# Feed-forward norm of an attention stack: token rows by two turnings instead of mean products, with the later steps moved back

## The chip, the cores and the metric

The kernel runs on one core of a Trainium2 chip. The metric is the device time of one execution in microseconds (us): 4307.7 us as the median of three runs (4302.38 to 4309.49).

## The reference

Eight modules work in turn on a residual x of 8 sequences of 256 tokens with 128 channels. Two of the eight are a stack of six layers, and nearly all of the time goes there. A layer of the stack is a local attention (16 heads of 64, windows of 32 keys) and a feed-forward block:

```
def shift_tokens(t):          # the upper 64 channels come from the token before
    a, s = jnp.split(t, 2, -1)
    s = jnp.pad(s, ((0, 0), (1, 0), (0, 0)))[:, :-1]
    return jnp.concatenate([a, s], -1)

def ffn_layer(x, g, bln, W1, b1, W2, b2):
    mu = x.mean(-1, keepdims=True)
    var = ((x - mu) ** 2).mean(-1, keepdims=True)
    xn = (x - mu) / jnp.sqrt(var + 1e-05) * g + bln
    hg = xn @ W1 + b1
    a, gate = jnp.split(hg, 2, -1)
    return a * jax.nn.gelu(gate, approximate=False) @ W2 + b2

for i in range(DEPTH):        # 6
    x = attn_layer(shift_tokens(x), Wqkv[i], q_scale[i], k_scale[i], Wo[i]) + x
    x = ffn_layer(shift_tokens(x), ln_g[i], ln_b[i], W1[i], b1[i], W2[i], b2[i]) + x
```

The change is in the first three lines of `ffn_layer`.

## The kernel before

Activations lie with the 128 channels on the partitions and the tokens along the row, in float32. The stack works on pairs of sequences, 512 tokens at a time: 4 pairs a layer, 6 layers, 2 calls, so 48 pairs. A pair takes eight steps, s = 0 to 7, and one step starts one unit, which is one sequence with one group of four heads. Every engine runs its own list of instructions, written out by hand in the `*_stack_step` functions, and engines wait for each other through the counters in `S`. Within a step the units are staggered: the step that starts unit s also carries unit s-2 (its rotated heads are turned), s-3 (scores and softmax) and s-4 (outputs).

TensorE (PE) does in a step, in this order: scores of s-3 (L291, L300), outputs of s-4 (L317), the turning of the heads of s-2 (L421, eight transposes, which wait for GpSimd's `rotated`), query and key products of s (L333, which wait for `scaled` of s-1), value products (L374), the turning of the probabilities (L406) and of the outputs (L391). In steps 3 and 7 the output projection (L361) follows.

What unit s needs before its heads can be turned two steps later runs through four engines: ScalarE (ACT) squares the products (L488), VectorE (DVE) sums them (L614), ACT makes the inverse length (L501, L504), DVE multiplies (L621, `scaled`), and GpSimd (POOL) rotates (L692, L694, L697, `rotated`).

The feed-forward block of a pair is fitted into the steps of the next one. A step has three places for it (`pe_stack_hidden`, `act_stack_hidden`, `dve_stack_hidden`, called with place 0, 1, 2), and `st.ffn(s)` says which step it is. On PE place 0 is before L333, place 1 after L374 and place 2 at the end of the step. On ACT place 0 is before L488, place 1 after the value copy L518 and place 2 at the end. On DVE place 1 is before L614 and place 2 at the end. Before the change:

- step 4: ACT copies the shifted tokens to `h.xc`; PE place 1 multiplies by `mean_w` (L433); DVE place 2 subtracts (L644); ACT place 2 squares (L551)
- step 5: PE place 0 takes the mean of the squares (L437); ACT place 0 makes the factor by Ln and Exp over 512 columns (L554, L556); DVE place 1 multiplies (L647); ACT place 2 applies gain and bias (L560)
- step 6: PE places 0, 1, 2 form the three gate products (L462), and ACT places 0, 1, 2 take them out (L565)
- step 7 and steps 0 to 2 of the next pair: gelu (L569, L571), value products, second product (L456), residual

All products of the block share PSUM bank 7. After the last pair of each call the block runs once more with nothing beside it (`*_stack_drain`).

Of the kernel before, what the change touches and what calls it, by code (L numbers as in the profile page):

```python
# [8 lines left out]
ALU = mybir.AluOpType  # L9
# [242 lines left out]
def stack_buffers(M):  # L252
# [4 lines left out]
                         total=(8,), inv=(8,), o=(8, DH), rs=(NB,)))  # L257


def stack_hidden(M):  # L260

    f = Parts()
    f.xc, f.gate = M.xc[:, 0:NB], M.xc[:, NB:4 * NB].rearrange("p (c t) -> p c t", c=3)
    f.sq, f.hid = M.ln_sq[:, 0, :], M.ln_sq[:, 1:4, :]
    f.rs = stack_buffers(M).rs
    f.ot = M.ln_rs[:].rearrange("p a t -> p (a t)").rearrange("p (g h t) -> p g h t", g=G, h=2)
    return f
# [158 lines left out]
def pe_stack_hidden(M, st, place):  # L426

    pe, S, w, h, s = st.eng, M.st, M.w, stack_hidden(M), st.s
    if st.ffn(4) and place == 1:
# [3 lines left out]
        pe.matmul(bank(M, 7), M.mean_w[:], h.xc, start=True, stop=True).then_inc(S.ffn_moment, 1)  # L433
    if st.ffn(5) and place == 0:
        done = st.ffn_done()
        pe.wait_ge(S.ffn_squared, done + 1)
        pe.matmul(bank(M, 7), M.mean_w[:], h.sq, start=True, stop=True).then_inc(S.ffn_moment, 1)  # L437
    if st.ffn(6):
        c = place
# [13 lines left out]
    if st.ffn(2) and place == 1:  # L453
# [3 lines left out]
        last.then_inc(S.ffn_out, 1)  # L457

# [80 lines left out]
def act_stack_hidden(M, st, place):  # L539
# [9 lines left out]
    if st.ffn(4) and place == 2:  # L549
        act.wait_ge(S.ffn_centred, st.ffn_done() + 1)  # L550
        nc.scalar.activation(h.sq, h.xc, ACT.Square).then_inc(S.ffn_squared, 1)  # L551
    if st.ffn(5) and place == 0:
        act.wait_ge(S.ffn_moment, st.ffn_done() * 2 + 2)
        nc.scalar.activation(h.rs, bank(M, 7), ACT.Ln, bias=M.eps[:, 0:1]).then_inc(S.ffn_scale, 1)  # L554
        act.wait_ge(S.ffn_scale, st.ffn_done() * 2 + 1)
        nc.scalar.activation(bank(M, 7), h.rs, ACT.Exp, scale=-0.5).then_inc(S.ffn_scale, 1)  # L556
    if st.ffn(5) and place == 2:
        act.wait_ge(S.w_ffn, 16 * 4 * (st.ffn_layer() + 1))
        act.wait_ge(S.ffn_normed, st.ffn_done() + 1)
        nc.scalar.activation(h.xc, h.xc, ACT.Identity, bias=w.vecs[:, 1:2], scale=w.vecs[:, 0:1]).then_inc(S.ffn_ready, 1)  # L560
    if st.ffn(6):
        c = place
# [4 lines left out]
    if st.ffn(7) and place == 1:  # L567
# [4 lines left out]
        nc.scalar.preload_act_table_set(NAT)  # L572

# [62 lines left out]
def dve_stack_hidden(M, st, place):  # L636
# [5 lines left out]
    if st.ffn(4) and place == 2:  # L642
        dve.wait_ge(S.ffn_moment, done * 2 + 1)
        nc.vector.tensor_tensor(h.xc, h.xc, bank(M, 7), ALU.subtract).then_inc(S.ffn_centred, 1)  # L644
    if st.ffn(5) and place == 1:
        dve.wait_ge(S.ffn_scale, done * 2 + 2)
        nc.vector.tensor_tensor(h.xc, h.xc, bank(M, 7), ALU.mult).then_inc(S.ffn_normed, 1)  # L647
# [59 lines left out]
def pe_stack_drain(M, pe, t):  # L707
# [3 lines left out]
    pe.matmul(bank(M, 7), M.mean_w[:], h.xc, start=True, stop=True).then_inc(S.ffn_moment, 1)  # L711
    pe.wait_ge(S.ffn_squared, t.done + 1)
    pe.matmul(bank(M, 7), M.mean_w[:], h.sq, start=True, stop=True).then_inc(S.ffn_moment, 1)
# [20 lines left out]
def act_stack_drain(M, act, t):  # L734
# [7 lines left out]
    act.wait_ge(S.ffn_centred, t.done + 1)  # L742
    nc.scalar.activation(h.sq, h.xc, ACT.Square).then_inc(S.ffn_squared, 1)
    act.wait_ge(S.ffn_moment, t.done * 2 + 2)
    nc.scalar.activation(h.rs, bank(M, 7), ACT.Ln, bias=M.eps[:, 0:1]).then_inc(S.ffn_scale, 1)
    act.wait_ge(S.ffn_scale, t.done * 2 + 1)
    nc.scalar.activation(bank(M, 7), h.rs, ACT.Exp, scale=-0.5).then_inc(S.ffn_scale, 1)
# [1150 lines left out]
```

## Time and profile before

| what | value |
|---|---|
| median of three runs | 4307.7 us |
| the profiled execution | 4315.31 us, span 4313.5 us |
| PE matmul busy | 3889.5 us (90%) |
| DVE busy | 2743.1 us (64%) |
| ACT busy | 2678.2 us (62%) |
| POOL busy | 3002.4 us (70%) |
| TensorE clock granted, 700 to 1800 us | 1.00 |

Busy times are shares of the whole span. Matmuls are pipelined, so a busy PE still has to be read from the starts of its instructions. In the timelines one row is a run of instructions of one line, with its start, its length from the first start to the last end, and in brackets how long the engine was idle before it and what ended that.

### The profile page before, as it was taken

To read this page: it belongs to the slowest core of one execution; us is meant where nothing else is said; L and a number is where in the kernel's file an instruction comes from. 1 tells how busy PE (TensorE), PEld (TensorE's weight loads), DVE (VectorE), ACT (ScalarE), POOL (GpSimd) and SP (SyncE) were. 2 spreads that over 40 slices of the span, in tenths; PEclk is the share of its full clock that TensorE was granted. 3 is DMA by queue.
4 is the path that set the end of the run, shared out by engine and by line. 5 is a ranking of instruction groups with operands and counts; after the bars stand their busy time and mean duration, and the time that the engine had idled before them with its cause. 6 is when DMAs were issued, how large, how long until landed. Compare 5 with 4: busy or idle time off the path is not lost.

```text
span 4313.5 us, 165583 instructions
## 1 busy us (share of the span) xinstructions
PE 3889.5 (90%) x69444; PEld 2741.9 (64%) x69444; DVE 2743.1 (64%) x4939; ACT 2678.2 (62%) x5554; POOL 3002.4 (70%) x1858
## 2 busy tenths in 40 slices
PE   7989999999999999977999999999999998375976
PEld 4556666766666767645666676767676765153645
DVE  5666766667676767645766666767676765624741
ACT  5657666676766767644666676767666675133752
POOL 0088888888888888825888888888888885611011
PEclk9999999999999999989999999999999999677987
DMA  2033433433334334312334343333433432040004
GB/s 69 2 83 92 110 97 96 111 93 104 104 93 108 99 102 105 91 54 53 95 101 105 89 112 95 102 106 94 109 99 95 111 93 57 0 114 19 2 13 128
DMA packets 349777, 367.29 MB, mean 85 GB/s; under 512 B 58737, under 2 KB 285298, under 8 KB 348786
## 3 DMA queue, kind: packets, MB, share of 16 engines
q1 hardware_dynamic: 338834, 348.59, 30.9%
q8 instruction: 555, 9.09, 0.9%
q0 software_dynamic: 2048, 4.20, 0.3%
q10 hardware_dynamic: 8160, 3.93, 0.3%
q14 instruction: 180, 1.47, 0.1%
HBM read 246.79 MB, written 109.71 MB: 83 GB/s over the span
## 4 chain that ended last, share of the span: by engine, by line
PE 39%; DVE 4%; ACT 3%; issue 3%; POOL 2%; DMA 1%; POOLq 0%; DVEq 0%; ACTq 0%
PE banks L333 6%; PE banks L361 4%; PE banks L374 4%; PE banks L421 3%; PE banks L462 3%; PE banks L317 3%; PE banks L300 2%; PE banks L406 2%; PE banks L391 2%; PE banks L456 1%; PE banks L1457 1%; ACT arena L1071 1%; PE banks L1477 1%; DVE arena L621 1%; PE banks L998 1%
## 5 line engine op out<-in xcount | busy, mean ns | idle before, releaser
L692 POOL TENSOR_TENSOR arena<-arena 128x512 f32<-128x512 f32 x768 | 959.5, 1270 | 394.0 <-DVE arena L621 253.6
L697 POOL TENSOR_TENSOR arena<-arena 128x1024 f32<-128x1024 f32 x384 | 905.9, 2359 | 30.1
L694 POOL TENSOR_TENSOR arena<-arena 128x1024 f32<-128x1024 f32 x384 | 908.1, 2365 | 0.0
L621 DVE SCALAR_TENSOR_TENSOR arena<-arena,banks 128x512 f32<-128x512 f32 x768 | 493.7, 684 | 508.7 <-ACT arena L504 502.1
L333 PE MATMUL banks<-w_qk,arena 128*128 128x512 f32 x1536 | 736.0, 602 | 16.4 <-DVE arena L797 10.6
L472 ACT COPY arena<-banks 128x512 f32<-128x512 f32 x384 | 224.5, 585 | 645.4 <-PE banks L421 645.2
L614 DVE TENSOR_REDUCE arena<-arena 128x8 f32<-128x512 f32 x768 | 487.6, 671 | 83.6 <-ACT arena L488 83.5
L488 ACT ACTIVATE arena<-banks 128x512 f32<-128x512 f32 x768 | 441.4, 593 | 66.3 <-PE banks L333 52.6
L333 PEld LDWEIGHTS banks<-w_qk,arena 128*128 128x128 f32 x1536 | 276.9, 193 | 272.5 <-issue 272.5
L421 PE MATMUL banks<-ident,arena 128*128 128x128 f32 x3072 | 423.1, 281 | 19.4 <-POOL arena L697 19.3
L588 DVE TENSOR_REDUCE arena<-banks 128x8 f32<-128x512 f32 x384 | 264.2, 688 | 212.6 <-PE banks L317 211.6
L374 PE MATMUL banks<-w_v,arena 128*128 128x256 f32 x1536 | 395.0, 380 | 0.0
L317 PE MATMUL banks<-arena 64*32 64x64 f32 x24576 | 341.8, 224 | 56.5 <-issue 55.4
L374 PEld LDWEIGHTS banks<-w_v,arena 128*128 128x128 f32 x1536 | 285.7, 191 | 160.8 <-issue 140.8
L421 PEld LDWEIGHTS banks<-ident,arena 128*128 128x128 f32 x3072 | 332.1, 142 | 56.0 <-POOL arena L697 21.9
L361 PE MATMUL banks<-ln_rs,w_o 128*128 128x256 f32 x1536 | 349.1, 380 | 1.4 <-ACT ln_rs L536 1.4
L317 PEld LDWEIGHTS banks<-arena 64*32 64x32 f32 x24576 | 280.0, 105 | 86.4 <-issue 67.3
L300 PE MATMUL banks<-arena 64*32 64x64 f32 x24576 | 325.3, 222 | 0.0
L526 ACT COPY arena<-banks 128x512 f32<-128x512 f32 x384 | 227.1, 591 | 148.9 <-PE banks L406 143.2
L361 PEld LDWEIGHTS banks<-ln_rs,w_o 128*128 128x128 f32 x1536 | 292.8, 191 | 42.0 <-ACT ln_rs L536 1.8
L604 DVE TENSOR_REDUCE arena<-arena 128x8 f32<-128x512 f32 x384 | 263.5, 686 | 64.5 <-ACT arena L481 24.5
L300 PEld LDWEIGHTS banks<-arena 64*32 64x32 f32 x24576 | 298.8, 105 | 0.2
(240 smaller groups left out, 6511.2 us busy)
## 6 DMA issues: line engine op xcount, KB each, us to landing
v_rows<-arena SPq DMA_DIRECT2D x1536, 64.0 KB
arena<-v_rows SPq DMA_DIRECT2D x768, 128.0 KB, 2.6
arena<-v_rows SPq DMA_DIRECT2D x768, 112.0 KB, 2.4
arena<-in_moe_w SPq DMA_DIRECT2D x30, 515.5 KB, 3.8
w_qk<-in_stack_qk SPq DMA_DIRECT2D x48, 256.0 KB, 3.0
w_v<-in_stack_v SPq DMA_DIRECT2D x48, 128.0 KB, 3.4
w_o<-in_stack_o SPq DMA_DIRECT2D x12, 512.0 KB
w_w<-in_stack_w SPq DMA_DIRECT2D x12, 341.0 KB, 3.1
```

The costliest lines, as they stand in the source:

```text
L300: last = pe.matmul(bank(M, 4 + par)[c:c + 32, o:o + KW], f.q[r, u % 2, hp, 32 * win:32 * win + 32], f.k[r, u % 2, hp, 32 * win:32 * win + ...
L317: last = pe.matmul(bank(M, 4 + par)[c:c + 32, o:o + DH], f.pt[r, win // 4, hp, c:c + 32], f.vb[r, u % 2, win, hp, :], start=True, stop=True)
L333: pe.matmul(bank(M, tile), f.sh[:, (s // G) % 2, o:o + 128], w.qk[:, g], start=True, stop=True).then_inc(S.qk, 1)
L361: last = pe.matmul(y, w.o[:, 2 * g + hp, :], stack_hidden(M).ot[:, g, hp, :], start=(g == 0 and hp == 0), stop=(g == G - 1 and hp == 1))
L374: last = pe.matmul(bank(M, 2)[:, 2 * D * tile:2 * D * tile + 2 * D], f.sh[:, (s // G) % 2, o:o + 128], w.v[:, g].rearrange("p a c -> p (a ...
L421: last = pe.transpose(bank(M, 2 if qk else 3)[:, o:o + 128], f.rot[:, u % 2, 2 * tile + qk, 2 * hp:2 * hp + 2, :], M.ident[:])
L488: nc.scalar.activation(f.sq[:, tile].rearrange("p h q d -> p (h q d)"), bank(M, tile), ACT.Square).then_inc(S.squared, 1)
L614: last = nc.vector.tensor_reduce(f.length[:, tile], f.sq[:, tile], AX.X, ALU.add)
L621: last = nc.vector.scalar_tensor_tensor(qn[:, :, tile], rn, 1e12, bank(M, tile).rearrange("p (h q d) -> p h q d", h=GH, q=2), ALU.min, ALU ...
L692: nc.gpsimd.tensor_tensor(f.sined[:, :, :, half, :], x[:, :, :, 1 - half, :], sines[:, :, mine].unsqueeze(1).to_broadcast([D, GH, 4, DH // ...
L694: nc.gpsimd.tensor_tensor(rot, x.rearrange("p h t a d -> p h t (a d)"), cosines.unsqueeze(1).to_broadcast([D, GH, 4, DH]), ALU.mult).then_ ...
L697: nc.gpsimd.tensor_tensor(rot, rot, f.sined.rearrange("p h t a d -> p h t (a d)"), ALU.add).then_inc(S.rotated, 1)
```

## The change

The norm is computed in token rows. PE turns the four blocks of 128 tokens of `h.xc` into rows (four transposes at the place of the first mean product). DVE reads them from bank 7 with four `bn_stats` and four `bn_aggr`, which give mean and variance of each token in a column. ACT makes the factor from 4 columns instead of 512. DVE writes the four normed blocks with one `tensor_scalar` each. PE turns them back at place 0 of step 6, and ACT applies gain and bias while it takes them out of bank 7. The gate products each move one place later: to places 1 and 2 of step 6 and place 0 of step 7. The square, the subtraction and both mean products go. The drains get the same operations in the same order.

```diff
@@ pe_stack_hidden
-        pe.matmul(bank(M, 7), M.mean_w[:], h.xc, start=True, stop=True).then_inc(S.ffn_moment, 1)
-    if st.ffn(5) and place == 0:
-        done = st.ffn_done()
-        pe.wait_ge(S.ffn_squared, done + 1)
-        pe.matmul(bank(M, 7), M.mean_w[:], h.sq, start=True, stop=True).then_inc(S.ffn_moment, 1)
-    if st.ffn(6):
-        c = place
+        pe_hidden_rows(M, pe)
+    if st.ffn(6) and place == 0:
+        pe.wait_ge(S.ffn_normed, st.ffn_done() + 1)
+        pe_hidden_turned(M, pe)
+    if st.ffn(6) and place > 0 or st.ffn(7) and place == 0:
+        c = (place + 2) % 3
...
+def pe_hidden_rows(M, pe):
+    h = stack_hidden(M)
+    for j in range(4):
+        last = pe.transpose(bank(M, 7)[:, 128 * j:128 * j + 128], h.xc[:, 128 * j:128 * j + 128], M.ident[:])
+    last.then_inc(M.st.ffn_rows, 1)
+
+
+def pe_hidden_turned(M, pe):
+    h = stack_hidden(M)
+    for j in range(4):
+        last = pe.transpose(bank(M, 7)[:, 128 * j:128 * j + 128], h.rows[:, j, :], M.ident[:])
+    last.then_inc(M.st.ffn_turned, 1)
@@ act_stack_hidden
-    if st.ffn(4) and place == 2:
-        act.wait_ge(S.ffn_centred, st.ffn_done() + 1)
-        nc.scalar.activation(h.sq, h.xc, ACT.Square).then_inc(S.ffn_squared, 1)
     if st.ffn(5) and place == 0:
-        act.wait_ge(S.ffn_moment, st.ffn_done() * 2 + 2)
-        nc.scalar.activation(h.rs, bank(M, 7), ACT.Ln, bias=M.eps[:, 0:1]).then_inc(S.ffn_scale, 1)
-        act.wait_ge(S.ffn_scale, st.ffn_done() * 2 + 1)
-        nc.scalar.activation(bank(M, 7), h.rs, ACT.Exp, scale=-0.5).then_inc(S.ffn_scale, 1)
-    if st.ffn(5) and place == 2:
+        act_hidden_factor(M, act, st.ffn_done())
+    if st.ffn(6) and place == 0:
         act.wait_ge(S.w_ffn, 16 * 4 * (st.ffn_layer() + 1))
-        act.wait_ge(S.ffn_normed, st.ffn_done() + 1)
-        nc.scalar.activation(h.xc, h.xc, ACT.Identity, bias=w.vecs[:, 1:2], scale=w.vecs[:, 0:1]).then_inc(S.ffn_ready, 1)
-    if st.ffn(6):
-        c = place
+        act.wait_ge(S.ffn_turned, st.ffn_done() + 1)
+        nc.scalar.activation(h.xc, bank(M, 7), ACT.Identity, bias=w.vecs[:, 1:2], scale=w.vecs[:, 0:1]).then_inc(S.ffn_ready, 1)
+    if st.ffn(6) and place > 0 or st.ffn(7) and place == 0:
+        c = (place + 2) % 3
...
+def act_hidden_factor(M, act, done):
+    S, h, nc = M.st, stack_hidden(M), M.nc
+    act.wait_ge(S.ffn_stats, done * 2 + 2)
+    nc.scalar.activation(h.factor, h.stats[:, :, 1], ACT.Ln, bias=M.eps[:, 0:1]).then_inc(S.ffn_scale, 1)
+    act.wait_ge(S.ffn_scale, done * 2 + 1)
+    nc.scalar.activation(h.factor, h.factor, ACT.Exp, scale=-0.5).then_inc(S.ffn_scale, 1)
@@ dve_stack_hidden: step 4, place 2
-        dve.wait_ge(S.ffn_moment, done * 2 + 1)
-        nc.vector.tensor_tensor(h.xc, h.xc, bank(M, 7), ALU.subtract).then_inc(S.ffn_centred, 1)
+        dve_hidden_stats(M, dve, done)
@@ dve_stack_hidden: step 5, place 1
-        dve.wait_ge(S.ffn_scale, done * 2 + 2)
-        nc.vector.tensor_tensor(h.xc, h.xc, bank(M, 7), ALU.mult).then_inc(S.ffn_normed, 1)
+        dve_hidden_scale(M, dve, done)
...
+def dve_hidden_stats(M, dve, done):
+    S, h, nc = M.st, stack_hidden(M), M.nc
+    dve.wait_ge(S.ffn_rows, done + 1)
+    for j in range(4):
+        last = nc.vector.bn_stats(h.parts[:, j], bank(M, 7)[:, 128 * j:128 * j + 128])
+    last.then_inc(S.ffn_stats, 1)
+    dve.wait_ge(S.ffn_stats, done * 2 + 1)
+    for j in range(4):
+        last = nc.vector.bn_aggr(h.stats[:, j], h.parts[:, j])
+    last.then_inc(S.ffn_stats, 1)
+
+
+def dve_hidden_scale(M, dve, done):
+    S, h, nc = M.st, stack_hidden(M), M.nc
+    dve.wait_ge(S.ffn_scale, done * 2 + 2)
+    for j in range(4):
+        last = nc.vector.tensor_scalar(h.rows[:, j, :], bank(M, 7)[:, 128 * j:128 * j + 128], h.stats[:, j, 0:1],
+                                       h.factor[:, j:j + 1], ALU.subtract, ALU.mult)
+    last.then_inc(S.ffn_normed, 1)
```

On PE, from the turning of the heads in step 6 (L421) to that in step 7, the list was this before the change:

```order
L421 MATMUL banks<-ident,arena 128x128 x8
L462 MATMUL banks<-xc,w_w 128x512
L333 MATMUL banks<-w_qk,arena 128x512 x2
L374 MATMUL banks<-w_v,arena 128x256 x2
L462 MATMUL banks<-xc,w_w 128x512
L406 MATMUL banks<-ident,arena 128x128 x4
L391 MATMUL banks<-ident,arena 128x128 x4
L462 MATMUL banks<-xc,w_w 85x512
L291 MATMUL banks<-wmask,identb 32x256 x8
L300 MATMUL banks<-arena 32x64 x32
L317 MATMUL banks<-arena 32x64 x32
L421 MATMUL banks<-ident,arena 128x128 x8
```

The same stretch of PE after the change, with the line numbers of the changed kernel (L470 is the second turning, L476 a gate product, L422 the turning of the heads), without its first row and with the first row of the step behind it:

```order
L470 MATMUL banks<-ident,ln_sq 128x128 x4
L334 MATMUL banks<-w_qk,arena 128x512 x2
L375 MATMUL banks<-w_v,arena 128x256 x2
L476 MATMUL banks<-xc,w_w 128x512
L407 MATMUL banks<-ident,arena 128x128 x4
L392 MATMUL banks<-ident,arena 128x128 x4
L476 MATMUL banks<-xc,w_w 128x512
L292 MATMUL banks<-wmask,identb 32x256 x8
L301 MATMUL banks<-arena 32x64 x32
L318 MATMUL banks<-arena 32x64 x32
L422 MATMUL banks<-ident,arena 128x128 x8
L476 MATMUL banks<-xc,w_w 85x512
```

One gate product has left the stretch for the step behind it, and four transposes have come in. On DVE, from the `scaled` of unit 4 (L621) to that of unit 5, before the change:

```order
L621 SCALAR_TENSOR_TENSOR arena<-arena,banks 128x4x128 x2
L644 TENSOR_TENSOR xc<-xc,banks 128x512
L588 TENSOR_REDUCE arena<-banks 128x8
L591 TENSOR_TENSOR arena<-banks,arena 128x512
L598 TENSOR_TENSOR arena<-banks,arena 128x512
L604 TENSOR_REDUCE arena<-arena 128x8
L607 RECIPROCAL arena<-arena 128x8
L647 TENSOR_TENSOR xc<-xc,banks 128x512
L614 TENSOR_REDUCE arena<-arena 128x8 x2
L621 SCALAR_TENSOR_TENSOR arena<-arena,banks 128x4x128 x2
```

The same stretch of DVE after the change (L637 is the former L621, L630 the former L614):

```order
L637 SCALAR_TENSOR_TENSOR arena<-arena,banks 128x4x128 x2
L679 BN_STATS arena<-banks 128x6 x4
L683 BN_AGGR arena<-arena 128x2 x4
L604 TENSOR_REDUCE arena<-banks 128x8
L607 TENSOR_TENSOR arena<-banks,arena 128x512
L614 TENSOR_TENSOR arena<-banks,arena 128x512
L620 TENSOR_REDUCE arena<-arena 128x8
L623 RECIPROCAL arena<-arena 128x8
L691 TENSOR_SCALAR ln_sq<-banks,arena 128x128 x4
L630 TENSOR_REDUCE arena<-arena 128x8 x2
L637 SCALAR_TENSOR_TENSOR arena<-arena,banks 128x4x128 x2
```

Eight small instructions stand where the subtraction stood, and four where the product with the factor stood.

## Rows read from the trace of the kernel before

**Rows 1.** Waits of PE, 700 to 1800 us: us in total, times, longest.

```profile
PE banks L317 <- issue: 17.1, 16, 1.6
```

**Rows 2.** Timeline of PE over steps 4 to 7 of one pair.

```profile
863.97 1.09 PE L421 MATMUL banks<-ident,arena 128*128 128x128 f32 x8
...
867.54 1.10 PE L433 MATMUL banks<-xc,mean_w 128*128 128x512 f32 x2
...
872.82 1.12 PE L437 MATMUL banks<-ln_sq,mean_w 128*128 128x512 f32 x2 [0.64 <-ACT ln_sq L551]
...
879.02 1.09 PE L421 MATMUL banks<-ident,arena 128*128 128x128 f32 x8
879.95 1.02 PE L462 MATMUL banks<-xc,w_w 128*128 128x512 f32 x2
880.81 1.88 PE L333 MATMUL banks<-w_qk,arena 128*128 128x512 f32 x4
...
887.86 1.09 PE L421 MATMUL banks<-ident,arena 128*128 128x128 f32 x8
...
897.45 1.09 PE L421 MATMUL banks<-ident,arena 128*128 128x128 f32 x8
```

**Rows 3.** Timeline of POOL in the same pair, units 4 and 5.

```profile
871.58 2.50 POOL L692 TENSOR_TENSOR arena<-arena 128x512 f32<-128x512 f32 x2 [2.42 <-DVE arena L621]
...
876.49 2.37 POOL L697 TENSOR_TENSOR arena<-arena 128x1024 f32<-128x1024 f32 x1
...
884.29 2.35 POOL L697 TENSOR_TENSOR arena<-arena 128x1024 f32<-128x1024 f32 x1
```

**Rows 4.** Timeline of ACT in the same pair, steps 4 and 5.

```profile
868.39 0.59 ACT L518 COPY arena<-banks 128x512 f32<-128x512 f32 x1
869.11 0.59 ACT L526 COPY arena<-banks 128x512 f32<-128x512 f32 x1
...
869.97 0.22 ACT L504 ACTIVATE arena<-arena 128x16 f32<-128x16 f32 x1
...
873.61 0.64 ACT L481 ACTIVATE arena<-arena 128x512 f32<-128x512 f32 x1
```

**Rows 5.** Timeline of DVE in the same pair, steps 4 and 5.

```profile
870.22 1.29 DVE L621 SCALAR_TENSOR_TENSOR arena<-arena,banks 128x512 f32<-128x512 f32 x2 [0.89 <-ACT arena L504]
871.42 0.68 DVE L644 TENSOR_TENSOR xc<-xc,banks 128x512 f32<-128x512 f32 x1
872.01 0.69 DVE L588 TENSOR_REDUCE arena<-banks 128x8 f32<-128x512 f32 x1
...
875.50 0.69 DVE L647 TENSOR_TENSOR xc<-xc,banks 128x512 f32<-128x512 f32 x1 [0.29 <-ACT banks L556]
876.10 1.27 DVE L614 TENSOR_REDUCE arena<-arena 128x8 f32<-128x512 f32 x2
878.02 1.28 DVE L621 SCALAR_TENSOR_TENSOR arena<-arena,banks 128x512 f32<-128x512 f32 x2 [0.65 <-ACT arena L504]
```

**Rows 6.** Groups by form, whole span: busy us, mean ns, then idle before.

```profile
L607 DVE RECIPROCAL arena<-arena 128x8 f32<-128x8 f32 x384 | 78.0, 203 | 13.4
...
L1155 DVE TENSOR_REDUCE arena<-banks 128x1 f32<-128x128 f32 x128 | 36.3, 284 | 34.7 <-PE banks L998 34.7
...
L1601 DVE TENSOR_SCALAR arena<-banks,arena 128x256 f32<-128x256 f32 x30 | 16.3, 544 | 103.4 <-PE banks L1467 103.4
```

**Rows 7.** Timeline of PE, stalls of the output products over two pairs.

```profile
751.24 0.33 PE L317 MATMUL banks<-arena 64*32 64x64 f32 x11 [0.99 <-issue]
...
777.78 0.34 PE L317 MATMUL banks<-arena 64*32 64x64 f32 x13 [1.13 <-issue]
...
796.67 0.55 PE L421 MATMUL banks<-ident,arena 128*128 128x128 f32 x3
...
804.58 0.38 PE L317 MATMUL banks<-arena 64*32 64x64 f32 x18 [0.87 <-issue]
...
811.88 0.33 PE L421 MATMUL banks<-ident,arena 128*128 128x128 f32 x1
```

More of the change, by code:

```diff
@@ L256, in stack_buffers @@
                          p=(8, KW), pt=(2, 2, 128), vt=(2, 2, 2, D), vb=(2, NW, 2, DH),
-                         total=(8,), inv=(8,), o=(8, DH), rs=(NB,)))
+                         total=(8,), inv=(8,), o=(8, DH), parts=(4, 6), stats=(4, 2), factor=(4,)))
 def stack_hidden(M):
@@ L263, in stack_hidden @@
     f.xc, f.gate = M.xc[:, 0:NB], M.xc[:, NB:4 * NB].rearrange("p (c t) -> p c t", c=3)
-    f.sq, f.hid = M.ln_sq[:, 0, :], M.ln_sq[:, 1:4, :]
-    f.rs = stack_buffers(M).rs
+    f.rows, f.hid = M.ln_sq[:, 0, :].rearrange("p (j c) -> p j c", j=4), M.ln_sq[:, 1:4, :]
+    own = stack_buffers(M)
+    f.parts, f.stats, f.factor = own.parts, own.stats, own.factor
     f.ot = M.ln_rs[:].rearrange("p a t -> p (a t)").rearrange("p (g h t) -> p g h t", g=G, h=2)
@@ L710, in pe_stack_drain @@
     pe.wait_ge(S.ffn_hi, t.done + 1)
-    pe.matmul(bank(M, 7), M.mean_w[:], h.xc, start=True, stop=True).then_inc(S.ffn_moment, 1)
-    pe.wait_ge(S.ffn_squared, t.done + 1)
-    pe.matmul(bank(M, 7), M.mean_w[:], h.sq, start=True, stop=True).then_inc(S.ffn_moment, 1)
+    pe_hidden_rows(M, pe)
+    pe.wait_ge(S.ffn_normed, t.done + 1)
+    pe_hidden_turned(M, pe)
     pe.wait_ge(S.w_ffn, 16 * 4 * (t.f // 4))
@@ L741, in act_stack_drain @@
     nc.scalar.copy(after, before).then_inc(S.ffn_hi, 1)
[L742 to L747, printed above, removed]
+    act_hidden_factor(M, act, t.done)
     nc.scalar.preload_act_table_set(GELU)
     act.wait_ge(S.w_ffn, 16 * 4 * (t.f // 4))
-    act.wait_ge(S.ffn_normed, t.done + 1)
-    nc.scalar.activation(h.xc, h.xc, ACT.Identity, bias=w.vecs[:, 1:2], scale=w.vecs[:, 0:1]).then_inc(S.ffn_ready, 1)
+    act.wait_ge(S.ffn_turned, t.done + 1)
+    nc.scalar.activation(h.xc, bank(M, 7), ACT.Identity, bias=w.vecs[:, 1:2], scale=w.vecs[:, 0:1]).then_inc(S.ffn_ready, 1)
     for c in range(3):
@@ L771, in dve_stack_drain @@
     nc.vector.tensor_tensor(x, x, z, ALU.add)
-    dve.wait_ge(S.ffn_moment, t.done * 2 + 1)
-    nc.vector.tensor_tensor(h.xc, h.xc, bank(M, 7), ALU.subtract).then_inc(S.ffn_centred, 1)
-    dve.wait_ge(S.ffn_scale, t.done * 2 + 2)
-    nc.vector.tensor_tensor(h.xc, h.xc, bank(M, 7), ALU.mult).then_inc(S.ffn_normed, 1)
+    dve_hidden_stats(M, dve, t.done)
+    dve_hidden_scale(M, dve, t.done)
     for c in range(3):
@@ L796, in dve_stack @@
         nc.vector.memset(f.vb[64 * par:64 * par + 32, :, 0], 0.0)
-    nc.vector.memset(f.rs, 0.0).then_inc(S.zeroed, 1)
+    nc.vector.memset(f.top, 0.0).then_inc(S.zeroed, 1)
     unit_steps(M, dve, m, dve_stack_step)
@@ L1720 @@
  maxed shifted probs summed inverted probs_turned probs_taken v v_taken v_stored v_loaded outs normed outs_turned
- outs_taken projected added ffn_lo ffn_hi ffn_moment ffn_centred ffn_squared ffn_scale ffn_normed ffn_ready gate_in gate_taken gated value_in hidden ffn_out state residual"""
+ outs_taken projected added ffn_lo ffn_hi ffn_rows ffn_stats ffn_scale ffn_normed ffn_turned ffn_ready gate_in gate_taken gated value_in hidden ffn_out state residual"""
 SINGLE_SIGNALS = """zeroed tok projected q k v q_masked scores maxed probs inverted normed turned pt pv residual"""
```

## The prediction

> **What bounds the kernel now.** I read the busy shares first: PE leads, so the next question is whether PE ever waits. The chain of waits for PE over sixteen pairs shows it idle mainly by itself: 17.1 us in 16 stalls in the output products L317, which nothing in the program explains ("issue") [rows 1]. Elsewhere PE runs its list back to back, so to first order a pair costs the sum of PE's starts, and any work added to PE costs its full length.
>
> There is one place where that is not so, and the change lies in it. I took PE's timeline from the turning of the heads (L421) in step 4 to that in step 6, 7 and 0 [rows 2]: 863.97, 879.02, 887.86 and 897.45, that is 15.05, 8.84 and 9.59 us. The first distance holds a wait of 0.64 us of L437 for ACT's square. Beside it I laid POOL [rows 3]: the rotation of unit 4 ends at 876.49 + 2.37 = 878.86, and the L421 that needs it starts 0.16 us later. So two chains end at that L421 together: PE's own, through the wait for the square, and the one over ACT, DVE and POOL that begins with the L421 of step 4. POOL had stood still for 2.42 us before that unit, waiting for DVE's `scaled`, and DVE for ACT [rows 3, 5]: the chain is a latency, not a full engine. One step later POOL ends at 884.29 + 2.35 = 886.64, 1.22 us before it is needed [rows 2, 3].
>
> I read the distance of the first two L421 in all 46 pairs that have the block between steps. In 30 it is 15.0 to 15.2; in 16 it is longer, by 0.36 on average, because one of the stalls of L317 falls into step 5. The pair at 796.67 is one of these: 811.88 - 796.67 = 15.21 [rows 7]. The other stalls fall in step 7 and step 2 of other pairs (751.24 and 777.78 are such a couple) [rows 7].
>
> **The change, part by part.** Prices on PE: one product of the block takes 880.81 - 879.95 = 0.86, and the eight transposes of L421 take 0.93, so four take 0.47 [rows 2]. The two mean products become two groups of four transposes: 2 x 0.47 - 2 x 0.86 = -0.78 us of PE work per pair. If PE alone decided, that and the 0.64 of waiting would be the gain. It does not, and I go through the pair in order.
>
> *Up to L421 of step 6.* PE loses 0.64 + 0.86 + (0.86 - 0.47) = 1.89 and could be there at 877.13, but POOL ends at 878.86 as before, unless its chain gets shorter. Of that chain ACT's part in step 4 keeps every instruction (the square stood behind it). One link moves: the copy L526 waits for the turned probabilities, which come 0.39 earlier. L518 ahead of it ends at 868.39 + 0.59 = 868.98, and L526 starts at 869.11 [rows 4], so at most 0.13 is to be had; below that the bound is nothing. I take 0.13: `scaled` at 870.09, POOL's end at 878.73, L421 at 878.89.
>
> *DVE between unit 4 and unit 5.* Instructions on DVE overlap by 0.09: L644 is 0.68 long and the next starts 0.59 later [rows 5]. No row shows `bn_stats`, `bn_aggr` or this `tensor_scalar`. For `bn_stats` the nearest is a sum over 128 columns of a bank, 0.284; for `bn_aggr` a small reciprocal, 0.203; for the `tensor_scalar` with two operands per row, 0.544 at 256 columns, and 0.284 as the floor at 128, so 0.41 between them [rows 6]. With the overlap: 4 x 0.19, then 0.09 because `bn_aggr` waits for the last `bn_stats`, then 4 x 0.11, is 1.3 us for 0.59 of L644; and 4 x 0.32 = 1.3 us for 0.60 of L647. Together +1.4. A wait of 0.29 + 0.09 before L647 goes, since ACT makes the factor with two small instructions of about 0.22 [rows 4] and it is ready before DVE asks: L481 comes 1.60 after L588 [rows 4, 5], now 874.2, and ends at 874.8, the factor is there at 875.3, DVE at 875.7. Net: +0.71 + 0.70 - 0.38 - 0.13 = +0.90 for L614 of unit 5, and with it for L621, 878.02 to 878.92 [rows 5].
>
> The Trainium skill, "VectorE: DVE Perf Modes", section on the TRN2 errata, speaks against this part: each instruction pays a fixed cost, so it advises tiles of 512 columns or more. From its table (120 cycles and one per column from PSUM at 0.96 GHz) I work out an estimate of 0.26 us for each of the eight instructions of 128 columns; with it the sum below would be about +23 instead of +21 us. The rows agree in kind, 0.284 for 128 columns beside 0.69 for 512 [rows 5, 6].
>
> *L421 of step 7.* POOL starts 1.36 after `scaled` and takes 7.28 [rows 3, 5]: 880.28 to 887.56, and with the 0.16 from POOL's end to L421 that is 887.72. PE's own way is 878.89 + 8.84 - 0.86 (a gate product leaves) + 0.47 (the second turning comes) = 887.34. POOL is later, so a new wait of 0.38 stands here, and L421 comes 0.14 before its old time.
>
> *Step 7.* It gets the third gate product: 9.59 + 0.86 = 10.45, and L421 of the next step 0 comes at 898.17 instead of 897.45. **+0.72 us per pair.** Nothing is queued there that hides it: PE works without a wait through steps 7 to 3. ACT's extra gate copy in step 7 costs nothing as long as it ends with PE's extra product; uncovered it would be at most one copy of about 0.6. GpSimd's and the DMA queue's lists do not change.
>
> *Sum.* 46 x 0.72 = 33. In the 16 pairs with a stall in step 5 the stall now hides behind POOL: -16 x 0.36 = -6. Where the stall falls in step 7, 0.38 of it hides behind the new wait: -16 x 0.38 = -6. The two drains run the same exchange with nothing beside it, shorter in some links and longer in others; I leave them at zero. Total **+21 us**, 0.5%. The profiled execution took 4315.31, 7.6 above the median; 4336 on its scale is **4329 us** on the median's.
>
> **Rivals.**
>
> *DVE's small instructions are cheap.* With `bn_stats` as short as the reciprocal (0.11 after overlap) and `tensor_scalar` at its floor (0.19), L614 moves by +0.06 only, POOL is done at 886.88 with its 0.16, and PE's own 887.34 decides: +0.34 per pair, 46 x 0.34 - 6 = +10, 4318. This and a little luck with the stalls is how "no change" comes about.
>
> *They are dear.* With 0.45 for each of the eight large ones and 0.19 for `bn_aggr`, L614 moves by +2.8, per pair +2.6, less 6 and the step 7 stalls that then hide whole (17): about +97, 4405. For this speaks that the nearest `tensor_scalar` row is 0.544; against it that its form has 256 columns. Half-way is 4367.
>
> *Faster: the stalls move away.* The stalls come back at the same lines every third pair, so they hang on the position in PE's instruction stream. A product is two loads and two matmuls, a transpose one of each (x2 for L433, x8 for the eight of L421 [rows 2]): 8 entries go, 16 come, a pair has 8 more, and the position drifts. The 16 stalls of 17.1 us in 16 pairs [rows 1] are 49 us in 46, of which 12 are counted above. If all the rest vanished, the result would be 21 - 37 = -16, 4292; it takes 30 of the 37 to be faster by 0.2%. They may as well become more by the same amount. No row shows the stream at another position, so I take zero.
>
> By the Trainium skill, "Runtime: NRT & Kernel Launch", section on instruction fetch, code arrives in blocks of 256 instructions and crossing a block is mostly hidden; by it neither stalls nor drift would count and the sum would be +33. The trace differs, with 17.1 us [rows 1].
>
> *Faster: POOL does not bind.* If something I do not see let POOL end with PE at 877.13, the pair would gain 1.42, and the time would be about 4240. The 0.16 between POOL and L421 speaks against it.
>
> **How the numbers follow.** The forecast (4310 to 4350) gets 0.5. Dear DVE work gets 0.16, cheap 0.2, vanishing stalls 0.11, POOL not binding 0.03. A measurement of this kernel tells changes of 0.2%, 8.6 us, from none. Cheap DVE work lies at the edge of that and goes mostly to "same"; faster 0.14, same 0.18, slower 0.68. The range runs from just above the case without stalls to half-way into dear DVE work, 4298 to 4368.
>
> **What would show it.** Right: L421 of step 6 starts within 0.2 of POOL's end in nearly all pairs, with PE idle by over a microsecond ahead of it; L421 of step 7 does so too; `scaled` of unit 5 comes 8.8 after that of unit 4 instead of 7.8; step 7 is 10.4 long. Wrong: POOL's unit 4 ending earlier by more than 0.2, four `bn_stats` and `bn_aggr` together under 1.0 or over 2.0, or the total of the L317 stalls away from 17 us in 1100 by more than half.

## The result and the profile after

The changed kernel takes 4346.3 us as the median of five runs (4344.8 to 4348.3); five of the kernel before gave 4307.7. The ratio is 1.0091, interval 1.0077 to 1.0106: about 39 us slower. I had forecast 4329 and +21. The line numbers of PE and ACT are up to 14 higher than before (the turning of the heads L421 is now L422, the output products L317 are L318), those of DVE 16 higher and of POOL 35.

The first line of the page, busy us of each engine:

```profile
PE 3860.4 (89%) x69636; PEld 2751.2 (63%) x69636; DVE 2800.5 (64%) x5419; ACT 2605.8 (60%) x5506; POOL 3002.1 (69%) x1858
```

PE has 29.1 us less to do than before (3889.5), and the kernel is longer: the time went into waits. The waits of 700 to 1800 us, in total us, times and longest:

```profile
PE banks L318 <- issue: 30.6, 26, 2.5
...
ACT arena L515 <- DVE arena L630: 16.2, 16, 1.1
...
PE banks L422 <- ACT ln_rs L550: 8.5, 8, 1.1
```

The first answers to [rows 1]: 17.1 us in 16 stalls have become 30.6 in 26. Of the second there was one wait of 0.3 us before (L501), and the third has no row that answers to it. A pair in which nothing stalls shows where they stand. PE's timeline, steps 4 to 7:

```profile
592.60 1.09 PE L422 MATMUL banks<-ident,arena 128*128 128x128 f32 x8
596.16 0.63 PE L463 MATMUL banks<-ident,xc 128*128 128x128 f32 x4
...
605.58 0.85 PE L318 MATMUL banks<-arena 64*32 64x64 f32 x64 [0.47 <-ACT arena L540]
607.57 1.06 PE L422 MATMUL banks<-ident,arena 128*128 128x128 f32 x8 [1.14 <-ACT ln_rs L550]
608.47 0.60 PE L470 MATMUL banks<-ident,ln_sq 128*128 128x128 f32 x4
...
615.99 1.09 PE L422 MATMUL banks<-ident,arena 128*128 128x128 f32 x8
...
626.44 1.09 PE L422 MATMUL banks<-ident,arena 128*128 128x128 f32 x8
```

From L422 to L422 that is 14.97, 8.42 and 10.45 us, where [rows 2] had 15.05, 8.84 and 9.59: **+0.36 us**, or 17 us in 46 pairs, with no stall in it. (It is the only one of the 46 pairs after the change that has none in these steps.) The first turning has its 0.46 and the second its 0.43 us.

POOL beside it, units 4 and 5, as in [rows 3]:

```profile
599.98 2.50 POOL L727 TENSOR_TENSOR arena<-arena 128x512 f32<-128x512 f32 x2 [2.19 <-DVE arena L637]
...
604.88 2.35 POOL L732 TENSOR_TENSOR arena<-arena 128x1024 f32<-128x1024 f32 x1
...
613.25 2.37 POOL L732 TENSOR_TENSOR arena<-arena 128x1024 f32<-128x1024 f32 x1
```

POOL ends at 607.23, 0.34 before the L422 of step 6, and at 615.62, 0.37 before that of step 7. DVE in the same pair, with its new instructions:

```profile
598.61 1.29 DVE L637 SCALAR_TENSOR_TENSOR arena<-arena,banks 128x512 f32<-128x512 f32 x2 [0.67 <-ACT arena L518]
599.82 0.89 DVE L679 BATCH_NORM_STATS2 arena<-banks 128x6 f32<-128x128 f32 x4
600.74 0.38 DVE L683 BATCH_NORM_AGGREGATE arena<-arena 128x2 f32<-128x6 f32 x4
601.03 0.66 DVE L604 TENSOR_REDUCE arena<-banks 128x8 f32<-128x512 f32 x1
...
603.95 1.32 DVE L691 TENSOR_SCALAR ln_sq<-banks,arena 128x128 f32<-128x128 f32 x4
605.18 1.27 DVE L630 TENSOR_REDUCE arena<-arena 128x8 f32<-128x512 f32 x2
606.98 1.28 DVE L637 SCALAR_TENSOR_TENSOR arena<-arena,banks 128x512 f32<-128x512 f32 x2 [0.53 <-ACT arena L518]
```

And ACT at the end of step 5:

```profile
606.49 0.21 ACT L515 ACTIVATE arena<-arena 128x16 f32<-128x16 f32 x1 [1.05 <-DVE arena L630]
...
606.86 0.57 ACT L550 COPY ln_rs<-banks 128x512 f32<-128x512 f32 x1
```

Here is the wait I had not seen. The heads of step 6 may be turned once ACT has copied the outputs of step 5 out of the bank (L550). In ACT's list that copy stands behind the logarithm of the lengths, L515, which waits for DVE's sums, L630. DVE's new work makes L630 late, and PE stands for 1.14 us, 0.8 of it with POOL still running.

The mean of the 44 distances between two L422 of step 0, over all pairs inside the two calls, is 68.24 us before and 69.10 after, +0.86. The 0.36 is the part without stalls; the rest, about 0.5 a pair or 22 us, I put down to the stalls. By stretch, the mean's excess over a pair without stalls grew by 0.13 us between the turnings of steps 4 and 6, by 0.28 between those of steps 6 and 7, and by 0.08 elsewhere.

### The profile page after: what moved, and what is told of

It is laid out like the page before. It is cut to its first block, busy times and chain, and to the rows that moved or that the text cites. A ratio compares the mean times of both kernels' runs of the same rounds, so it can differ in the third digit from the quotient of the medians.

```text
span 4344.3 us, 166399 instructions
## 1 busy us (share of the span) xinstructions
PE 3860.4 (89%) x69636; PEld 2751.2 (63%) x69636; DVE 2800.5 (64%) x5419; ACT 2605.8 (60%) x5506; POOL 3002.1 (69%) x1858
## 4 chain that ended last, share of the span: by engine, by line
PE 36%; DVE 5%; ACT 5%; issue 4%; POOL 2%; DMA 1%; SPq 0%; POOLq 0%; ACTq 0%; DVEq 0%
PE banks L334 5%; PE banks L362 4%; PE banks L422 3%; PE banks L375 3%; PE banks L476 3%; PE banks L318 3%; PE banks L301 2%; PE banks L407 2%; PE banks L392 1%; PE banks L456 1%; PE banks L1485 1%; ACT arena L1099 1%; PE banks L1505 1%; DVE arena L637 1%; PE banks L1026 1%
## 5 line engine op out<-in xcount | busy, mean ns | idle before, releaser
L637 DVE SCALAR_TENSOR_TENSOR arena<-arena,banks 128x512 f32<-128x512 f32 x768 | 493.6, 684 | 486.0 <-ACT arena L518 476.5
L630 DVE TENSOR_REDUCE arena<-arena 128x8 f32<-128x512 f32 x768 | 489.6, 673 | 97.9 <-ACT arena L502 97.3
L422 PE MATMUL banks<-ident,arena 128*128 128x128 f32 x3072 | 427.4, 282 | 50.6 <-ACT ln_rs L550 23.4
L318 PE MATMUL banks<-arena 64*32 64x64 f32 x24576 | 343.9, 224 | 104.2 <-issue 89.6
L422 PEld LDWEIGHTS banks<-ident,arena 128*128 128x128 f32 x3072 | 335.1, 142 | 91.5 <-POOL arena L732 47.0
L318 PEld LDWEIGHTS banks<-arena 64*32 64x32 f32 x24576 | 279.7, 105 | 139.7 <-issue 121.8
L495 ACT ACTIVATE arena<-arena 128x512 f32<-128x512 f32 x384 | 244.4, 636 | 109.8 <-DVE arena L607 108.7
```

The lines of the kernel that those rows point to most:

```text
L318: last = pe.matmul(bank(M, 4 + par)[c:c + 32, o:o + DH], f.pt[r, win // 4, hp, c:c + 32], f.vb[r, u % 2, win, hp, :], start=True, stop=True)
L422: last = pe.transpose(bank(M, 2 if qk else 3)[:, o:o + 128], f.rot[:, u % 2, 2 * tile + qk, 2 * hp:2 * hp + 2, :], M.ident[:])
L630: last = nc.vector.tensor_reduce(f.length[:, tile], f.sq[:, tile], AX.X, ALU.add)
L637: last = nc.vector.scalar_tensor_tensor(qn[:, :, tile], rn, 1e12, bank(M, tile).rearrange("p (h q d) -> p h q d", h=GH, q=2), ALU.min, ALU ...
```

## The experiments

Kernels named a_ start from the changed kernel, those named b_ from the one before. Ratios are to the kernel before on the same chip, so those of a_ kernels are read against 1.0091.

**Are the longer stalls the list's new length?** The pairs have eight entries more on PE, so the stalls wander through the steps. b_pad8 adds eight empty entries to the kernel before; a_drop8 takes eight from the changed one.

```
     if st.ffn(5) and place == 0:               # b_pad8
         done = st.ffn_done()
+        for _ in range(8):
+            pe.sem_inc(M.s.pe_waited)
         pe.wait_ge(S.ffn_squared, done + 1)
...
         st.wait(S.normed, u)                   # a_drop8, ahead of the output products
-        pe.sem_inc(M.s.pe_waited)
```

> The kernel before, with eight entries per pair that do no work (semaphore increments) added to TensorE's list at the start of step 5, ahead of the wait for the squares where TensorE stands idle for over 1 us in the trace of before. The changed kernel also has eight entries per pair more there. Stream theory (the longer issue stalls of the changed kernel come from the list's new length per pair, by which the stalls wander through the steps): 4322 to 4335 us, and the stalls of the output products between 700 and 1800 us grow from 17.1 us to 25 us or more, spread over more steps. Work theory (the stalls grew because the new work stands elsewhere): 4305 to 4311 us, the stalls near 17 us.

> The changed kernel with one of the two semaphore increments per step taken from TensorE's list (the one ahead of the output products), so that a pair has as many entries as before the change; the work is the same. Stream theory: the stalls of the output products fall from 30.6 us between 700 and 1800 us to near 17 us, at the same steps in every third pair, and the time falls by about 20 us to 4318 to 4335 us. Work theory: 4342 to 4348 us.

b_pad8: 4317.9 us, ratio 1.0029 (1.0018 to 1.0039). a_drop8: 4348.1 us, 1.0099 (1.0084 to 1.0115). The stalls, b_pad8 first, then a_drop8:

```profile
PE banks L317 <- issue: 16.9, 20, 1.3
...
PE banks L421 <- issue: 1.7, 3, 1.0
```

```profile
PE banks L317 <- issue: 40.6, 32, 1.8
```

As I had stated it the stream theory falls: with the new length the old kernel's output products stall as before, and with the old length the changed kernel's stall more, not less. But the length is not free. b_pad8 lost 14 us, about a third of what the change lost, which neither theory had. Its pairs without a stall from step 4 to the next step 0 are no longer than before (33.47 us in the mean of 10, before 33.55 of 14), so the loss lies in the pairs that stall, some at a line that had no stall before (the second row), and not in the entries' own length. a_drop8 is not clean either, since the entry that it takes away was not free where it stood: the first output product starts 0.02 us behind the last score product in most steps, and 0.13 in the changed kernel. Its mean pair is 0.45 us shorter from the turning of step 7 to that of step 4, and 0.44 longer from there to step 7, where the stalls grew. So its time stayed because two effects cancel.

**What does the turning of step 6 wait for?** a_outs_first puts ACT's copy of the outputs ahead of the logarithm in step 5. a_shift_early puts the two token copies of step 4 at the head of ACT's step, into 4.7 us of idle time.

```
         act_stack_probs(M, st)                 # a_outs_first
+    if s == 5:
+        act_stack_outs(M, st)
     if st.on(0):
         ...                                    # Ln and Exp of the lengths
-    else:
+    elif s != 5:
         act_stack_outs(M, st)
...
+    act_hidden_shift(M, st)                    # a_shift_early: the block ffn(4), place 0
     if st.on(2):
         ...                                    # copies of the turned heads
```

> The changed kernel with ScalarE's copy of the turned outputs in step 5 put ahead of the logarithm of the lengths, which waits for VectorE there. Outs theory (the turning of the heads in step 6 waits for this copy): the wait of 8.5 us in 8 times between 700 and 1800 us goes, GpSimd's addition becomes what the turning meets 0.34 us earlier, and the time falls by 6 to 16 us, to 4330 to 4340 us. GpSimd theory (what the prediction said: GpSimd's addition sets this place): 4343 to 4349 us, the wait is only renamed.

> The changed kernel with ScalarE's two token copies of step 4 put ahead of its copies of the turned heads, in ScalarE's 4.7 us of idle time, so that the squares of unit 4 start up to 0.8 us earlier. Chain theory (the span from the turning of step 4 to that of step 6 is set by ScalarE, VectorE and GpSimd in turn): step 5 or 6 gets 0.5 to 0.8 us shorter in each of 46 pairs, 4308 to 4325 us. Rival (TensorE's own list and its stalls take the place at once): 4338 to 4348 us.

a_outs_first: 4335.0 us, 1.0071 (1.0058 to 1.0085). a_shift_early: 4321.0 us, 1.0034 (1.0022 to 1.0046). Both theories that named the place hold, though the 9 us of a_outs_first are a difference of two ratios whose intervals still overlap. In a_outs_first the wait has a new releaser and is shorter, 6.4 us for 8.5:

```profile
PE banks L422 <- POOL arena L734: 6.4, 8, 0.9
```

So ACT's copy was last, and POOL comes right behind it.

**Do the gate products cost, or the second turning?** b_gates_late makes one part of the change alone. a_turn_first puts the second turning into the time that PE waits anyway.

```
-    if st.ffn(6):                              # b_gates_late, on PE and on ACT
-        c = place
+    if st.ffn(6) and place > 0 or st.ffn(7) and place == 0:
+        c = (place + 2) % 3
...
+    if st.ffn(6):                              # a_turn_first, gone from place 0
+        pe.wait_ge(S.ffn_normed, st.ffn_done() + 1)
+        pe_hidden_turned(M, pe)
     if st.on(2):
         pe_stack_heads(M, st, 0)
```

> The kernel before with one part of the change alone: the three gate products stand at the places 1 and 2 of step 6 and 0 of step 7, as in the changed kernel; the norm stays as it was. Give-and-take theory: step 6 is made of TensorE's own work and gives the 0.86 us of one product back (8.84 to 8.0 us, GpSimd ends 1.2 us ahead of the turning of step 7 and so is not met), step 7 gets 0.85 us longer (9.59 to 10.44 us), and the sum is nothing: 4298 to 4312 us. What makes the changed kernel slower would then be its second turning in step 6, 0.43 us, and not the gate products. Rival (the place of the third gate product is what costs, since step 6 can't give all of it back): step 6 stays above 8.4 us, 4318 to 4330 us.

> The changed kernel with its second turning moved, in TensorE's list, from behind the turning of the heads in step 6 to ahead of it, where TensorE stands 1.14 us for ScalarE's copy and GpSimd in a pair without stalls; the normalized rows are there 1.1 us before that place. Placement theory (the change is slower since the second turning's 0.43 us stands in step 6 behind that wait): step 6 goes from 8.43 to 8.0 us, the wait before it shrinks by as much, and the time falls by 15 to 20 us, to 4326 to 4332 us. Rival (step 6 can't give it back, since GpSimd holds the turning of step 7 as the prediction said): 4342 to 4348 us.

b_gates_late: 4312.4 us, 1.0006 (0.9997 to 1.0015): nothing, as give-and-take had it. The turnings of steps 6, 7 and 0:

```profile
879.17 1.09 PE L421 MATMUL banks<-ident,arena 128*128 128x128 f32 x8
...
887.19 1.09 PE L421 MATMUL banks<-ident,arena 128*128 128x128 f32 x8
...
897.64 1.09 PE L421 MATMUL banks<-ident,arena 128*128 128x128 f32 x8
```

Step 6 is 8.02 and step 7 10.45 us long: 0.82 given, 0.86 taken. a_turn_first: 4337.0 us, 1.0072 (1.0059 to 1.0085), about half of what I expected, and again with overlapping intervals. The wait shrinks as it should, from 8.5 to

```profile
PE banks L425 <- ACT ln_rs L550: 4.3, 8, 0.6
```

but only in the pairs that wait. Where the stall of step 6 has already used up the wait, the turning adds its length in front of the heads instead.

**Why does step 6 stall now?** The page of the changed kernel has the pieces of PE's list in a queue of their own (packets, MB, share):

```profile
q8 instruction: 556, 9.11, 0.9%
```

2 x 69636 loads and products with some 3400 semaphore entries make 256 entries a piece. The small products of a step, L292 to L318, are 16 + 128 + 128 entries in 1.7 us. My second theory was that PE asks for a piece when its sequencer passes into the one ahead, that a wait not yet met holds the sequencer, and that the piece then comes too late for entries that go so fast. a_wait5 holds PE earlier, where the kernel before held it; a_stats_late gives the probabilities to PE sooner.

```
+    if st.ffn(5) and place == 0:               # a_wait5
+        pe.wait_ge(S.ffn_stats, st.ffn_done() * 2 + 2)
+        pe.sem_inc(M.s.pe_waited)
...
                                 ALU.mult).then_inc(S.normed, 1)
+    if st.ffn(5):                              # a_stats_late, gone from ffn(4), place 2
+        dve_hidden_stats(M, dve, st.ffn_done())
```

> The changed kernel with one wait and one semaphore entry added to TensorE's list at place 0 of step 5, where the kernel before waited for the squares: it now waits there for VectorE's statistics, about 0.9 us, in time that it otherwise waits later in steps 5 and 6. Timing theory (the output products of step 6 stall since TensorE, no longer held at this place, comes to step 6 too early, is held there just ahead of the small products, and has the list's next piece too late): the stalls of step 6, 24 in the whole run against 2 before the change, fall below 8, and the time by 3 to 12 us to 4334 to 4343 us. Rival (the stalls come from where the entries stand in the list): they stay above 15, and the time is 4345 to 4352 us.

> The changed kernel with VectorE's statistics moved behind its scores, shifts and divided outputs of step 5, so that the probabilities of step 5 are there about 1 us before TensorE wants them, not 0.05 us. Read-ahead theory (the list's next piece is asked for only when TensorE's sequencer has passed the wait for the probabilities, which the statistics delay): the fetches come earlier, the stalls of step 6 fall from 24 (32.6 us in the run) to below 10, and the time falls by 5 to 15 us, to 4331 to 4341 us. Rival (the stalls of step 6 have another cause in the new list): they stay above 18, and the time is 4343 to 4350 us.

a_wait5: 4339.6 us, 1.0065 (1.0052 to 1.0079), with 23 stalls of step 6 in the run, for 24. The time came out as the timing theory said, and its reason did not: the stalls stayed. Where the 11 us come from I could not find; the mean pair of its profile is no shorter (69.06 us), and this run's interval, too, overlaps that of the changed kernel. a_stats_late: 4350.3 us, 1.0096 (1.0082 to 1.0111). The stalls of step 6 went to 13, 10.9 us for 32.6 (counted from one product's start to the next), not below the 10 of the read-ahead theory, and the time stayed. DVE now has the sums later, and another wait grew:

```profile
PE banks L318 <- issue: 21.2, 22, 1.7
...
PE banks L318 <- ACT arena L540: 11.6, 15, 1.0
```

The second row had 3.8 us in 9 in the changed kernel. The two rows together are 32.8 us, and were 34.4: the wait now stands in the steps that lost their stall, so this run can't tell an earlier fetch from a stall that the wait covers. It shows no gain.

**The norm alone, at the old places.** a_early is the other part of the change.

```
-    if st.ffn(6) and place == 0:               # second turning (PE) and affine (ACT)
+    if st.ffn(5) and place == 2:
...
-    if st.ffn(6) and place > 0 or st.ffn(7) and place == 0:
-        c = (place + 2) % 3
+    if st.ffn(6):                              # gate products, PE and ACT
+        c = place
```

> The changed kernel with the places of before: its second turning and the affine stand at place 2 of step 5, where the affine stood, and the three gate products at the places 0, 1 and 2 of step 6; only the norm in token rows and its factor are new. Norm theory (the token-row norm itself makes the pair longer: its chain over VectorE and ScalarE ends 1.1 us after TensorE has done its list of step 5, so that TensorE has to wait wherever the second turning stands): steps 4 and 5 together 15.3 to 15.6 us against 15.0 us of both kernels, step 6 8.84 us, step 7 9.59 us, and 4338 to 4362 us, no faster than the changed kernel. Rival (the later places are what costs): 4308 to 4328 us.

4358.7 us, 1.0118 (1.0101 to 1.0135). The time is in the range of the norm theory, but the reason I gave is wrong again: in a pair without stalls in these steps nothing is lost. Its turnings of steps 4, 6, 7 and 0:

```profile
2256.49 1.09 PE L422 MATMUL banks<-ident,arena 128*128 128x128 f32 x8
...
2271.47 1.09 PE L422 MATMUL banks<-ident,arena 128*128 128x128 f32 x8
2280.31 1.09 PE L422 MATMUL banks<-ident,arena 128*128 128x128 f32 x8
2289.90 1.09 PE L422 MATMUL banks<-ident,arena 128*128 128x128 f32 x8
```

14.98, 8.84 and 9.59: 33.41 us, where [rows 2] had 33.48. The mean pair is 69.7 us all the same (in a profiled execution that took 17.5 us more than the median). Of the 1.5 us over the kernel before, 0.77 lie between the turnings of steps 4 and 6 and 0.64 between those of steps 6 and 7. The second part I have not followed. The first goes with the stall that comes behind the new wait at the end of step 5:

```profile
674.03 0.66 PE L470 MATMUL banks<-ident,ln_sq 128*128 128x128 f32 x4 [0.62 <-DVE ln_sq L691]
674.61 0.30 PE L292 MATMUL banks<-wmask,identb 64*32 64x256 bf16 x8
674.73 0.84 PE L301 MATMUL banks<-arena 64*32 64x64 f32 x64
675.49 0.45 PE L318 MATMUL banks<-arena 64*32 64x64 f32 x28
677.90 0.60 PE L318 MATMUL banks<-arena 64*32 64x64 f32 x36 [1.96 <-issue]
```

The traffic between 675.3 and 675.5 us holds one piece of PE's list; from 670 to 675.3 there is none:

```profile
q8 instruction: 1, 0.02, 38.9%
```

The piece starts 0.7 to 0.9 us after the small products do, and they go on 2.4 to 2.6 us after its start. The kernel before, in the pair of [rows 2], has in step 6 one piece between 876.2 and 876.4 us and none from 873 to 879.1 beside it:

```profile
q8 instruction: 1, 0.02, 29.2%
```

Its small products of step 6 begin at 877.32, a microsecond later, and do not stall. This is the same step and the same small products, and the fetch stands on the other side of their start. The whole traces say the same. Counted in loads, products and semaphore entries, all stalls of the output products, 56 before the change and 80 after, stand at one of two neighbouring numbers modulo 256 in each call: there the next piece is needed. Such a place falls into the output products of step 6 in 31 pairs before the change, and one of them stalls; it falls there in 23 pairs after the change, and all 23 stall. In the 30 the fetch had started 0.7 to 4.4 us ahead of the small products, in the 23 between 0.9 ahead and 1.7 behind their start. So step 6 stalls because the fetch comes later, and not by the place alone.

Why it comes later is not proved. In a_early DVE's L691 releases PE 0.64 us ahead of the small products in all 46 pairs; of the 23 with such a place the 20 that stall have their fetch behind the start of the small products, the other 3 at least 1.4 us ahead. That fits a wait that holds the fetch back, but no run moves this wait alone, and other traffic was not tried as a cause. For the changed kernel's own step 6 the cause is open: a_wait5 did not remove the stalls, and a_stats_late may only have covered them.

Nor are these stalls where most of the time went. They have 27 us of idle time in the changed kernel, but in the stretch from step 4 to step 6 the excess over a pair without stalls grew by only 0.13 us, 6 us in 46 pairs: no pair that stalls in step 6 has the full wait of 1.14 us behind it, so the stall mostly stands in for that wait.

**Can the chain be shortened?** a_comb has the moves of a_shift_early and a_outs_first and, in step 4, the logarithm and exponential of the lengths ahead of the copy of the probabilities; b_comb is the kernel before with the first and the third of these; a_comb_turn adds the edit of a_turn_first to a_comb.

```
         act_stack_hidden(M, st, 1)
+        if s == 4:
+            act_stack_lengths(M, st)           # Ln and Exp, else behind it
         act_stack_probs(M, st)
```

> The changed kernel with three moves in ScalarE's list: the token copies of step 4 ahead of the copies of the heads, the logarithm and exponential of the lengths in step 4 ahead of the copy of the probabilities, and the copy of the turned outputs of step 5 ahead of the logarithm. Chain theory: GpSimd starts unit 4 about 1 us earlier, the outputs are copied in time, and the 1.1 us that the turning of step 6 waits in a pair without stalls goes down to 0.1 us: 4294 to 4310 us. Rival (the stalls of TensorE's list eat most of it, or VectorE is late next): 4312 to 4322 us.

> The kernel before with two of these moves in ScalarE's list: the token copies of step 4 ahead of the copies of the heads, and the logarithm and exponential of the lengths in step 4 ahead of the copy of the probabilities. Chain theory: VectorE's scaling of unit 4 starts up to 1 us earlier, so do the centring, the squares and GpSimd, and the wait of 0.64 us for the squares in a pair without stalls goes: 4270 to 4292 us, faster than before. Rival (the kernel before is bound by TensorE's own work there): 4298 to 4308 us.

> The changed kernel with the three moves in ScalarE's list and the second turning ahead of the heads, together. If the two gains add: 4270 to 4278 us, near the 4264 us of the kernel before with its two moves. If GpSimd or the stalls take the place of the second: 4282 to 4292 us.

a_comb: 4290.5 us, 0.9956 (0.9942 to 0.9969). b_comb: **4264.1 us, 0.9890 (0.9875 to 0.9905)**, faster than both kernels. a_comb_turn: 4293.9 us, 0.9965 (0.9953 to 0.9977), no more than a_comb. The first two came out faster than the ranges that I had given them, and the third just above both of its ranges. What is left in a_comb is POOL; the turnings of steps 4, 6, 7 and 0 of a pair:

```profile
586.68 1.09 PE L422 MATMUL banks<-ident,arena 128*128 128x128 f32 x8
...
600.43 1.09 PE L422 MATMUL banks<-ident,arena 128*128 128x128 f32 x8 [0.86 <-POOL arena L746]
...
608.89 1.09 PE L422 MATMUL banks<-ident,arena 128*128 128x128 f32 x8
...
619.37 1.09 PE L422 MATMUL banks<-ident,arena 128*128 128x128 f32 x8
```

13.75 us of chain, in which PE still stands for 0.86. b_comb's PE does not wait there at all:

```profile
652.83 1.09 PE L421 MATMUL banks<-ident,arena 128*128 128x128 f32 x8
...
666.85 1.09 PE L421 MATMUL banks<-ident,arena 128*128 128x128 f32 x8
...
675.69 1.09 PE L421 MATMUL banks<-ident,arena 128*128 128x128 f32 x8
...
685.29 1.09 PE L421 MATMUL banks<-ident,arena 128*128 128x128 f32 x8
```

14.02 us with its longer mean products and no wait ahead of them. So most of the 0.78 us that the two turnings save on PE lies where the chain sets the pace: of it 0.27 reaches the pair, and steps 6 and 7 take 0.50 back (8.46 and 10.48 us for 8.84 and 9.60). The mean pairs of the two are 67.91 and 67.14 us; 0.23 of this is without stalls, and the rest I again put down to stalls.

## Why the prediction was right, and where not

- **Two chains meet at the turning of step 6: right.** Steps 4 and 5 kept their length (14.97 for 15.05) though PE's list lost over a microsecond of work and waiting there, and moving ACT's token copies alone was worth 25 us. But POOL ends 0.34 before that turning, not the 0.2 that I had named as the sign: a third chain ends behind it. And POOL's unit 4 ends 0.26 us earlier (14.63 us behind the turning of step 4, before 14.89), a little more than the 0.2 that I had named as a sign of being wrong.
- **The prices: nearly right.** DVE's statistics take 601.03 - 599.82 = 1.21 us (predicted 1.3) and the scaling 605.18 - 603.95 = 1.23 (1.3). POOL's chain for unit 4 is 0.24 shorter (6.25 to 6.01 us from turning to `scaled`; I took 0.13). The estimate from the Trainium skill, "VectorE: DVE Perf Modes", section on the TRN2 errata, 0.26 us for each 128 columns, lies below the rows: 284 ns for the statistics and 393 for the scaling. The +23 that I had worked out from it is wrong: it leaves out the overlap of 0.09 that my other prices have, and with it PE's own list would have set the turning of step 7, about +10. `scaled` of unit 5 comes 606.98 - 598.61 = 8.37 after that of unit 4; I wrote 8.8, before it was 7.80.
- **"POOL is later, so a new wait of 0.38 stands here": this step failed.** I summed the small errors of DVE on one side. POOL ends 0.37 ahead of the turning of step 7, whose time is PE's own: 8.42 us, which I had worked out (8.84 - 0.86 + 0.47 = 8.45). The new wait stands one step earlier, at the turning of step 6, and belongs to ACT's copy of the outputs, behind a logarithm that DVE makes late. I had followed DVE's delay to POOL and not along ACT's list.
- **+0.72 us a pair: mis-sized.** Without stalls it is +0.36: 0.08 less from step 4 to 6, 0.42 less in step 6, 0.86 more in step 7. Step 7 grew as said. The gate product's move is neutral, as b_gates_late shows; what stays is the second turning in step 6, 0.43 us.
- **"-6" and "-6" for the stalls, and zero for their drift: this step failed, and by most.** The stalls grew from 17.1 to 30.6 us in 1100, beyond the bound that I had set for being wrong. Instead of giving 12 us back they go with about 22 more. The rival in which the drift makes them vanish was wrong too, and zero for the drift is not borne out: eight more entries alone, b_pad8, cost 14 us. "Mostly hidden", as the Trainium skill has it in "Runtime: NRT & Kernel Launch", section on instruction fetch, agrees with the count of crossings (437 of 488 inside the pairs before the change go without a stall, 404 of 490 after); the trace shows the others as stalls.
- **"The two drains ... at zero": nearly.** From the first turning to the last, the two calls are 19.3 and 20.5 us longer, the profiled span only 30.8, so the rest is 9 us shorter. The drains have 3.2 of it: with nothing beside it, the way from the first token copy to the first gate product took 9.52 and 8.68 us before and takes 7.52 in both now. In the first drain, before and after:

```profile
1877.41 0.62 ACT L738 COPY xc<-z 64x512 f32<-64x512 f32 x1 [4.39 <-DVE xc L770]
...
1886.93 7.76 PE L719 MATMUL banks<-xc,w_w 128*128 128x512 f32 x12 [3.63 <-ACT xc L751]
```

```profile
1898.67 0.62 ACT L773 COPY xc<-z 64x512 f32<-64x512 f32 x1 [4.39 <-DVE xc L800]
...
1906.19 8.36 PE L754 MATMUL banks<-xc,w_w 128*128 128x512 f32 x12 [1.02 <-ACT xc L781]
```

So the new norm by itself is shorter, and what it loses it loses beside the other work of the pair. The other 6 us I have not followed.

That the total came within 18 us is luck, since two errors stood against each other: 33 was too much by 16, and -12 should have been +22.

## What to carry to other kernels

When work is added to one engine, follow the delay along every in-order list that waits for it, not only along the data's own chain: here the copy that held PE up had nothing to do with the norm. Work saved on the busiest engine counts only where no other chain ends with it, and added work costs most where none does; moving four short instructions within ACT's list brought 1.1%, more than the new norm brought in any run here.

## What the runs showed of the hardware

A piece of PE's list that is fetched late has a price. The list comes in pieces of 256 entries, and where PE stalled for one, the next product started 2.2 to 2.9 us after the start of the fetch, in nine of ten stalls before and after the change. The small products of a step take 272 entries in 1.7 us. A fetch that started 0.7 to 0.9 us into such a run left PE idle for 1.96 us; one that started 1 us ahead of it cost nothing. In a_early a wait of 0.62 us stood just ahead of the run that stalled, but 26 of its 46 pairs are released at the same place and do not stall, so the wait alone is not the price.

An entry that only counts up a semaphore is not always free: taken from between the score and the output products (a_drop8), it shortened the distance from one to the other from 0.13 to 0.02 us in most steps, while eight of them ahead of a wait (b_pad8) added nothing to a pair without stalls.
